# A vision block on one core: the opening's products, its copies, and the last choice of experts put in another order

## The chip, the cores and the metric

The program runs on one core of one Trainium2 chip. The metric is device time in microseconds (us) of one execution, lower being better. Times of single instructions come from one profiled execution.

## The reference

A tokeniser, one attention layer and one mixture-of-experts layer run over 32 images of 36 patches, so 1152 tokens of width 192.

```python
y = einsum('bchw,rc->bhwr', x, W_repr) + b_repr          # 3 channels to 5 representations
h = einsum('rbnp,rep->bne', patches(y), W_proj) + b_proj.sum(0)
h = h + attention(layernorm(h))                          # 12 heads of 64, 36 tokens an image, softmax(8 q.k)
xt = layernorm(h)
gates = softmax(xt @ gate_w + gate_b); expert = argmax(gates)      # 8 experts
out = h + (gelu(xt @ w1[e] + b1[e]) @ w2[e] + b2[e] of the chosen expert)
```

## The kernel before, in words

Each engine has its own instruction stream, written out by hand, and waits on semaphores; an engine works in order. A helper `own(ins)` makes DVE wait until its own instruction has written its result, and is used wherever the next one reads it. The tokens are nine tiles of 128, in three blocks of three tiles. Attention goes by units of two images (72 tokens), 16 in all.

- **Opening.** SP loads the projection weights, three tiles of x (`xb`), and the attention weights in pieces. DVE and ACT fold the 3-to-5 channel mix into one effective weight per channel: `weff[0]` by DVE alone, `weff[2]` and `weff[1]` from products that ACT scales. PE computes a bias row (`bias`), copied out by ACT. Then PE lays the bias into the accumulators of the three tiles (L667) and adds the channels 0, 2, 1 (L674). DVE takes the statistics of each tile (L1221 to L1223), POOL the reciprocal root (L1553), DVE normalises (L1125), PE turns the tile (L511, L512), ACT rounds it to fp32r (L939, L940) and copies its lower rows once more (L942), DVE takes the rest of the rounding (L1152, L1153). Then come the twelve query and key products of block 0 (L523). In between PE multiplies small columns for the gate (L681, L689), and transposes of the identity (`keep_clock`, L646), whose results nobody reads, fill its waits. ACT also rounds the weight pieces (`round_wqA`, L917, and `round_wqB`, L922), and DVE splits off the remainder (L1159, L1165).
- **Blocks.** The functions `middle_block` of PE, ACT and DVE interleave the units' attention of a block with the tokenising, turning and products of the next. PE may only turn the probabilities of a unit (`turn_probs`, L574) when ACT has copied those of the unit before (`take_probs`, L978).
- **Last block.** When a tile's attention is done, PE projects it (L603); DVE adds the residual into `rows` (L1279) and the gate logits into `raw` (L1280), takes statistics, and normalises it (`finish_row`, L1125). Rows go to a table in HBM by DMA; the last tile is normalised by ACT (L1066), which also issues two DMAs (L1069): three tiles, then one. DVE chooses the expert of four tiles at once (`gate_logits`, L1307 and L1317, and `choose_experts`, L1330 to L1336), PE ranks the tokens (L612 to L628), DVE turns ranks into slots (L1352 to L1370, L1440), PE makes the token lists (L636), DVE writes them as integers (`ids`, L1445).
- **Experts.** POOL waits for the rows in the table and for `ids`, then gathers tokens by list (L1565), 16 tiles of 128. PE turns a gathered tile (`turn_x`, L838 and L839), multiplies up (`up`, L849 first half, L856 second half) and down (L878); `more_lists` (L829) makes the lists of the tiles 8 to 15. ACT does the gelu, DVE the copies.

## Time and profile before

| | us |
|---|---|
| three executions | 240.25, 242.35, 243.03; median 242.35 |
| the profiled execution | 241.82 |
| its span in the trace | 240.1 |
| TensorE busy in it | 223.4 (93%) |

The span runs from the first to the last instruction in the trace; the 1.7 us that the profiled execution's time is longer lie around it. A row of a timeline or chain begins with the time from the start of the span and the duration.

### The profile page before, as it was taken

How to read it: one execution, taken by the hardware profiler on the slowest of the kernel's cores; microseconds unless marked ns; L12 is line 12 of the kernel's file. 1: busy time of each engine (PE TensorE's matmuls, PEld its weight loads, DVE VectorE, ACT ScalarE, POOL GpSimd, SP SyncE). 2: the span in 40 equal slices, each digit the busy share in tenths (PEclk: the TensorE clock that was granted, in tenths of full speed). 3: DMA queues.
4: the chain of work that ended last, by engine and by line, in shares of the span. 5: the costliest groups of instructions: out<-in, count | busy, mean ns of one | idle time of the engine just before them, and what ended most of it. 6: DMA issues, size and time to landing. Idle time of an engine off the chain costs nothing.

```text
span 240.1 us, 7756 instructions
## 1 busy us (share of the span) xinstructions
PE 223.4 (93%) x3238; PEld 206.1 (86%) x3238; DVE 121.5 (51%) x390; ACT 116.1 (48%) x309; POOL 53.4 (22%) x84
## 2 busy tenths in 40 slices
PE   6999999998999999899998899789999999999990
PEld 5898998887999888799977789679999999999980
DVE  1878236993431798447289737872324324324310
ACT  2765555547265637544556650305235546646220
POOL 8201000021110012023000021170354354353131
PEclk9999799999999999999999999999999999999998
DMA  5999962325054240500813533331112212311000
GB/s 183 332 238 360 413 256 62 105 67 175 3 194 169 68 127 9 203 1 30 284 52 88 139 132 101 132 107 59 48 49 64 85 49 53 79 47 48 3 0 0
DMA packets 10055, 27.70 MB, mean 115 GB/s; under 512 B 2333, under 2 KB 4921, under 8 KB 9380
## 3 DMA queue, kind: packets, MB, share of 16 engines
q1 hardware_dynamic: 7636, 22.28, 28.9%
q0 software_dynamic: 1840, 4.13, 6.2%
q10 hardware_dynamic: 544, 0.79, 0.9%
q8 instruction: 26, 0.43, 0.7%
q14 instruction: 9, 0.07, 0.1%
HBM read 21.00 MB, written 3.34 MB: 101 GB/s over the span
## 4 chain that ended last, share of the span: by engine, by line
PE 74%; DVE 11%; DMA 4%; ACT 3%; issue 3%; POOL 1%; SPq 1%; DVEq 0%; POOLq 0%
PE psum L523 19%; PE psum L878 13%; PE psum L849 9%; PE psum L603 8%; PE psum L856 6%; PE psum L587 4%; PE psum L556 3%; PE psum L574 3%; DMA w1s<-xT 3%; PE psum L504 3%; PE psum L674 2%; DVE kT L1177 2%; DVE top L1176 2%; PE psum L838 2%; ACT w2s L978 1%
## 5 line engine op out<-in xcount | busy, mean ns | idle before, releaser
L878 PE MATMUL psum<-w2s,kT 128*128 128x192 f32 (+1 forms) x192 | 33.8, 327 | 0.0
L523 PE MATMUL psum<-xn_hi,wq_parts 128*128 128x384 f32 x108 | 32.2, 353 | 0.3 <-DVE w_r L1153 0.3
L878 PEld LDWEIGHTS psum<-w2s,kT 128*128 128x128 f32 x192 | 30.8, 190 | 0.1
L1552 POOL TENSOR_SCALAR veps<-mv 128x1 f32<-128x1 f32 x15 | 3.3, 221 | 116.9 <-DVE mv L1122 116.9
L1097 ACT ACTIVATE kT<-psum,w1s 128x128 f32<-128x128 f32 x48 | 13.2, 375 | 26.1 <-PE psum L856 26.1
L1576 POOL DMA_INDIRECT out<-oT,ids x16 | 16.2, 1010 | 42.9 <-DVE oT L1499 42.9
L523 PE MATMUL psum<-w_r,wq_parts 128*128 128x384 f32 x72 | 25.2, 350 | 0.0
L1481 DVE COPY qT<-psum 128x128 f32<-128x128 f32 x16 | 4.7, 291 | 33.3 <-PE psum L839 33.3
L1097 ACT ACTIVATE kT<-psum,late 128x128 f32<-128x128 f32 x48 | 13.2, 375 | 16.7 <-PE psum L856 16.7
L523 PEld LDWEIGHTS psum<-xn_hi,wq_parts 128*128 128x128 f32 x108 | 20.9, 197 | 0.4 <-ACT xn_hi L942 0.4
L603 PE MATMUL psum<-wo,oT 128*128 128x200 f32 x108 | 20.4, 339 | 0.5 <-issue 0.5
L603 PEld LDWEIGHTS psum<-wo,oT 128*128 128x128 f32 x108 | 18.0, 190 | 1.1 <-issue 0.6
L1176 DVE TENSOR_REDUCE top<-psum 100x12 f32<-100x432 f32 x16 | 9.6, 602 | 17.8 <-PE psum L556 17.5
L1565 POOL DMA_INDIRECT wq_in<-token_table,ids x16 | 15.7, 981 | 10.2 <-DVE ids L1445 5.5
L523 PE MATMUL psum<-wq_parts,xn_hi 128*128 128x384 f32 (+1 forms) x54 | 17.0, 369 | 0.6 <-issue 0.6
L646 PE MATMUL psum<-ident 128*128 128x128 f32 x102 | 14.1, 295 | 2.2 <-POOL ident L1526 1.8
L955 ACT ACTIVATE kT<-kT 100x432 f32<-100x432 f32 x16 | 9.0, 563 | 12.4 <-DVE kT L1177 11.7
L949 ACT COPY qT<-psum 128x384 f32<-128x384 f32 (+4 forms) x30 | 9.4, 354 | 11.6 <-PE psum L523 11.6
L646 PEld LDWEIGHTS psum<-ident 128*128 128x128 f32 x102 | 12.5, 152 | 2.5 <-POOL ident L1526 1.8
L523 PEld LDWEIGHTS psum<-w_r,wq_parts 128*128 128x128 f32 x72 | 14.1, 196 | 0.0
L949 ACT COPY kT<-psum 128x384 f32<-128x384 f32 (+4 forms) x30 | 9.4, 354 | 9.3 <-PE psum L523 9.3
L1499 DVE TENSOR_TENSOR oT<-psum,oT 128x192 f32<-128x192 f32 x16 | 5.7, 358 | 15.8 <-PE psum L878 15.8
(176 smaller groups left out, 447.3 us busy)
## 6 DMA issues: line engine op xcount, KB each, us to landing
w1s<-w_b SPq DMA_DIRECT2D x1, 3474.0 KB, 13.6
w1s<-xT SPq DMA_DIRECT2D x9, 384.0 KB, 4.5
late<-wq_in SPq DMA_DIRECT2D x24, 108.0 KB
w2s<-w SPq DMA_DIRECT2D x2, 1152.0 KB, 7.1
w2s<-w SPq DMA_DIRECT2D x1, 1728.0 KB, 7.0
w1s<-w_b SPq DMA_DIRECT2D x1, 1158.0 KB, 5.2
late<-w_proj SPq DMA_DIRECT2D x2, 480.0 KB, 4.0
b2s<-b SPq DMA_DIRECT2D x1, 768.0 KB, 15.0
```

Of the source, the lines that this page charges most:

```text
L523: mm = pe.matmul(dst, lhsT, rhs, start=(i == 0), stop=(i == len(parts) - 1))
L587: mm = pe.matmul(dst[DH * k:DH * (k + 1), c * GT:(c + 1) * GT], v[0:SPAN, u % V_SLOTS, j * DH:(j + 1) * DH], probsT[u % 2][:, j * GT:(j + ...
L603: mm = pe.matmul(dst[0:TT, 0:D + EXPERTS], oT[:, c, at:at + TT], wo[:, c, :], start=(c == 0), stop=(c == PAIRS - 1))
L646: pe.transpose(psum[:, bank, 0:P], ident[:, :], ident[:, :])
L849: pe.matmul(psum[:, 2 * p2 + c % 2, at:at + SLOT], w[:, c * P:(c + 1) * P], fxA[p2], start=(c < 2), stop=False)
L856: mm = pe.matmul(psum[:, 2 * p2 + c % 2, at:at + SLOT], w[half, FF + at:FF + at + P], fxB[p2][half, :], start=False, stop=(c >= FCH - 2))
L878: mm = pe.matmul(psum[:, Y_BANKS[j % 2], 0:D], hidT[j % 2][:, c * P:(c + 1) * P], w[:, :, c, :], start=(c == 0), stop=(c == FCH - 1))
L949: cp = act.copy((qT if w == "q" else kT)[:, c, to], acc(slot[0])[:, tokens])
L1097: ge = act.activation(hidT[p2][:, c * P:(c + 1) * P], psum[:, 2 * p2 + c % 2, c // 2 * P:(c // 2 + 1) * P], ACT.Gelu, bias=w1_of(j)[:, UP ...
L1176: own(dve.tensor_reduce(most, sc, AX.X, ALU.max))
L1565: pool.indirect_dma_start(out=xg[j % 4], out_offset=None, in_=table, in_offset=bass.IndirectOffsetOnAxis(ap=ids[:, j:j + 1], axis=0)).then ...
L1576: pool.indirect_dma_start(out=out, out_offset=bass.IndirectOffsetOnAxis(ap=ids[:, j:j + 1], axis=0), in_=yo[j % 4], in_offset=None, bounds ...
```

## The change

It reorders work in three places.

1. **Opening.** A tile of x has a semaphore of its own (`x_first[t]`), and channel 0 of a tile waits for that tile only. Four of the filling transposes go. The first matmul into an accumulator is now channel 0's; the bias is laid in between channel 2 and channel 1. The gate columns are spread between the turns of the three tiles (2, 2, 2 instead of 0, 2, 4). On ACT, rounding the lower rows of weight piece 1 (`round_wqB(1)`) moves from before the tokens to behind the copies of the turned tiles, and the doubled lower rows (`double_xnB`, the old L942) come one step later, behind the next tile's two copies.
2. **Middle blocks.** The same doubling comes behind the next `take_probs`. In every `take_o` DVE takes the statistics before the gate logits instead of behind them.
3. **The last block.** The choice of experts is made in three parts: tiles 0 and 1 together, before the third projection is ready, then tile 2, then tile 3. ACT normalises tile 2 as well as tile 3, so `shift` has two columns. The ranking of the block before (`place_tokens`) is taken apart and laid into waits. `ids` is written before the three small instructions that make slots (`slots_in_tiles`). In the experts' start, the second tile is turned inside the first `up`, between its halves, instead of before it.

The core of the diff:

```diff
             for t in range(NT):
-                sp.dma_start(xb[:, t, :, :], xT[t]).then_inc(x_here, 16)
+                sp.dma_start(xb[:, t, :, :], xT[t]).then_inc(x_first[t], 16)
...
-            pe.wait_ge(x_here, 16 * NT)
-            pe.wait_ge(sc_free, 1)
-            keep_clock(4, TR_BANK)
-            taken(pe, product("bias"))
-            for t in range(NT):
-                pe.matmul(into(product("tok", t))[0:TT, 0:D], ident[0:TT, 0:TT], bias[:, :],
-                          start=True, stop=False)
-            for c in (0, 2, 1):
+            def channel(c):
                 pe.wait_ge(weff_ready[c], 1)
                 for t in range(NT):
                     slot = product("tok", t)
+                    if c == 0:
+                        into(slot)
+                        pe.wait_ge(x_first[t], 16)
                     for i in range(2):
                         mm = pe.matmul(acc(slot[0])[0:TT, 0:D], xb[:, t, 2 * c + i, :],
-                                       weff[:, c, i, :], start=False, stop=(c == 1 and i == 1))
+                                       weff[:, c, i, :], start=(c == 0 and i == 0), stop=(c == 1 and i == 1))
...
+            channel(0)
+            channel(2)
+            taken(pe, product("bias"))
+            for t in range(NT):
+                pe.matmul(acc(product("tok", t)[0])[0:TT, 0:D], ident[0:TT, 0:TT], bias[:, :], start=False, stop=False)
+            channel(1)
...
             keep_clock(10, TR_BANK)
             turn_tokens(0)
-            turn_tokens(1)
             pe.wait_ge(gw_here, 48)
             pe.wait_ge(woT_here, 48)
             gate_columns(0, 2)
+            turn_tokens(1)
+            gate_columns(2, 4)
             turn_tokens(2)
-            gate_columns(2, PAIRS)
+            gate_columns(4, PAIRS)
...
+            def second_turn_and_lists():
+                turn_x(1)
+                more_lists()
             turn_x(0)
             keep_clock(6, TR_BANK)
-            turn_x(1)
-            up(0, more_lists)
+            up(0, second_turn_and_lists)
...
-            for i in range(2):
-                round_wqA(i)
-                round_wqB(i)
+            round_wqA(0)
+            round_wqB(0)
+            round_wqA(1)
...
+            def double_xnB(t):
+                toks = slice(t % NT * TT, (t % NT + 1) * TT)
                 act.wait_ge(xn_hi_ready, t + 1)
                 act.copy(xnB[DB:2 * DB, toks], xnB[0:DB, toks]).then_inc(xnB_ready, 1)
...
-            for t in range(NT):
-                take_xn_hi(t)
+            take_xn_hi(0)
+            take_xn_hi(1)
+            double_xnB(0)
+            take_xn_hi(2)
+            double_xnB(1)
+            double_xnB(2)
+            round_wqB(1)
...
-                for i0, i1 in ((0, NG - 1), (NG - 1, NG)):
-                    if i1 == NG:
-                        act.wait_ge(shift_ready, 1)
-                        act.activation(rows[:, i0, D:2 * D], rows[:, i0, 0:D], ACT.Identity, bias=shift[:, :],
-                                       scale=rstd[:, 1, i0:i0 + 1]).then_inc(rows_ready, 1)
+                for k, (i0, i1) in enumerate(((0, NG - 1), (NG - 1, NG))):
+                    act.wait_ge(shift_ready, k + 1)
+                    act.activation(rows[:, i1 - 1, D:2 * D], rows[:, i1 - 1, 0:D], ACT.Identity,
+                                   bias=shift[:, k:k + 1], scale=rstd[:, 1, i1 - 1:i1]).then_inc(rows_ready, 1)
...
                 take_o(r)
+                tiles_of_tokens(b - 1)
                 finish_row(r)
                 take_o(r + 1)
+                own(slots_of_tokens(b - 1))
+                centre_logits(b, 0, 2)
+                dve.sem_inc(small_free, 1)
                 finish_row(r + 1)
-                place_tokens(b - 1)
+                own(scale_logits(b, 0, 2))
+                choose_experts(b, 0, 2)
                 take_o(r + 2)
                 take_o(r + 3)
-                finish_row(r + 2)
-                gate_logits(b)
-                choose_experts(b)
+                normed(1, r + 2)
+                shift_of(n - 2)
+                centre_logits(b, 2, 4)
+                own(scale_logits(b, 2, 3))
+                choose_experts(b, 2, 3)
+                ins = scale_logits(b, 3, 4)
+                own(ins)
+                shift_of(n - 1)
+                choose_experts(b, 3, 4)
+                dve.sem_inc(onehot_ready, 1)
...
-                tiles_of_tokens(b)
+                count_tiles(b)
                 dve.wait_ge(ids_full, 1)
                 dve.tensor_scalar(ids[:, 0:EXPERTS], psum[:, IDS_BANK, 0:EXPERTS], -1.0, float(TOKENS), ALU.mult,
                                   ALU.add).then_inc(ids_ready, 1)
+                slots_in_tiles(b)
```

`rank_tokens(b - 1)` now stands before the last `soften`. `centre_logits` is the first loop of the old `gate_logits` for some of the tiles (L1307), `scale_logits` the second (L1317), and `shift_of` the old `shift` instruction (L1313) for one tile. `count_tiles` is L1365 and L1367; `slots_in_tiles` is L1368 to L1370. In `take_o` the addition into `rows` is now waited for, the statistics follow, and the logits' addition, which frees the accumulator, is last.

## Rows read from the trace of the kernel before

**Rows 1.** The page, the chain that ended last: shares by engine

```profile
PE 74%; DVE 11%; DMA 4%; ACT 3%; issue 3%; POOL 1%; SPq 1%; DVEq 0%; POOLq 0%
```

**Rows 2.** The chain in order of time (start, us, what): opening, and block 1's products

```profile
11.85 4.56 PE psum L674 x28
...
22.16 12.32 PE psum L523 x60
...
65.08 11.43 PE psum L523 x65
```

**Rows 3.** Timeline of DVE, opening: start, us, operation, then idle and its releaser

```profile
7.09 2.58 DVE L1203 SCALAR_TENSOR_TENSOR w2s<-late,wr_br,w2s 128x384 f32<-128x384 f32 x4
...
11.16 0.56 DVE L1215 TENSOR_TENSOR w2s<-w2s 128x384 f32<-128x384 f32 x1
...
13.82 0.56 DVE L1215 TENSOR_TENSOR w2s<-w2s 128x384 f32<-128x384 f32 x1
...
15.01 0.69 DVE L1165 TENSOR_TENSOR wq_parts<-wq_in,wq_parts 64x512 fp32r<-64x512 f32 x1
...
19.41 0.38 DVE L1125 TENSOR_SCALAR rows<-h,mv,rstd 128x192 f32<-128x192 f32 x1 [0.22 <-POOL rstd L1553]
...
21.64 0.27 DVE L1153 TENSOR_TENSOR w_r<-psum,xn_hi 64x128 fp32r<-64x128 f32 x1
```

**Rows 4.** Timeline of ACT, opening

```profile
15.96 1.04 ACT L922 CAST wq_parts<-wq_in 64x1024 fp32r<-64x1024 f32 x1
...
21.43 0.30 ACT L942 CAST xn_hi<-xn_hi 64x128 fp32r<-64x128 f32 x1
```

**Rows 5.** Timeline of PE, opening

```profile
10.21 0.66 PE L646 MATMUL psum<-ident 128*128 128x128 f32 x4 [0.39 <-DMA w1s<-xT]
...
18.96 0.33 PE L511 MATMUL psum<-ident,rows 128*128 128x128 f32 x1 [0.17 <-DVE rows L1125]
...
20.14 0.96 PE L681 MATMUL psum<-gwA,w2s 128*128 128x8 f32 x8
```

**Rows 6.** DMA issues around 9.8 us: size, us from issue to landing

```profile
w2s<-w_outT SPq DMA_DIRECT2D x2, 96.0 KB, 7.5
```

**Rows 7.** Busy times of a stretch; behind POOL's the granted clock

```profile
23.00:27.00 4.00, 4.00 (x16) 4.00 (x15) 1.26 (x2) 1.44 (x3) 0.00 (x0) 0.57 1.11 450
```

**Rows 8.** Timeline of all engines, second middle block

```profile
95.78 0.65 PE L574 MATMUL psum<-ident,kT 36*36 36x36 f32 x48
...
96.75 1.04 ACT L978 COPY late<-psum 36x432 f32<-36x432 f32 x2
...
97.93 0.64 PE L574 MATMUL psum<-ident,kT 36*36 36x36 f32 x48 [0.61 <-ACT late L978]
```

**Rows 9.** The chain in order of time, first middle block and the last block's end

```profile
55.76 0.49 issue
...
148.53 0.36 DVE rows L1279
...
152.69 0.20 DVE onehots L1336
...
154.94 0.17 DVE none L1368
...
155.38 0.09 DVE ids L1445
...
155.53 0.74 issue
```

**Rows 10.** Timeline of ACT, last block's end

```profile
151.60 0.34 ACTq L1069 DMA_DIRECT2D token_table<-rows  x1
```

**Rows 11.** DMA issues from 148 to 166 us: size, us from issue to landing

```profile
token_table<-rows ACTq DMA_DIRECT2D x1, 192.0 KB, 2.8
```

**Rows 12.** Timeline of PE, the experts' start

```profile
159.92 0.82 PE L646 MATMUL psum<-ident 128*128 128x128 f32 x6
160.80 0.33 PE L838 MATMUL psum<-ident,wq_in 128*128 128x128 f32 x1
```

94 lines of the change are left out of this document (54 added, 40 removed).

## The prediction

> **What bounds the kernel now.** I read the page's chain first: TensorE carries 74% of it [rows 1]. So an edit pays only where PE waits or does work that goes away. I then followed the chain in order of time and marked where it leaves PE. In the opening it goes over PE's products (to 16.41), then statistics, turning and rounding, until the twelve query and key products begin at 22.16 [rows 2]. In the middle blocks it crosses ACT's copies of the probabilities [rows 8]. In the last block, from 148.53, it runs over DVE, POOL and a DMA until the first gather starts at 155.53 + 0.74 = 156.27 [rows 9]. From 161 us on PE does the experts without a gap, so whatever the experts start earlier is kept to the end. The three edits touch these three places.
>
> **The opening.** What is removed: four filling transposes, and PE's wait for all of x (0.39 us idle to 10.21, so PE was free at 9.82) [rows 5]. Channel 0 needs `weff[0]`, ready at 7.09 + 2.58 = 9.67 [rows 3], and one tile of x at a time, the last at 10.21. Its first product starts at about 9.8. A product of 192 columns is two instructions of 4.56 / 28 = 0.163 us [rows 2]. Channel 0 takes 12 of them, to 11.76, just behind `weff[2]` at 11.72; channel 2 goes to 13.72; the bias (6 instructions) to 14.70, past `weff[1]` at 13.82 + 0.56 = 14.38 [rows 3]. Moving the bias between the channels so covers that wait; without it PE would stand 0.66 us. Four instructions of channel 1 finish tile 0 at 14.70 + 0.65 and a tail of about 0.16, 15.5; before it was 16.41 [rows 2]. The products are 0.9 us earlier, but now DVE is late: it splits a weight piece until 15.70 [rows 3] and can begin the statistics there, 0.03 later than its work allows at most. Statistics began at about 16.44, so the gain is 0.74 to 0.76; tiles 1 and 2 are ready 0.65 us apart and DVE takes 0.68 for each, so it stays so. ACT would have been the next thing late: it rounds `round_wqB(1)` until 17.00 [rows 4], and must copy tile 0 at about 16.5. That is what moving this rounding is for; it is worth 0.5 us of the 0.76.
>
> The third normalising ran from 19.41 [rows 3]; it moves to 18.65, and the first turn from 18.96 [rows 5] to 18.2. Then the new order on PE: two turns' instructions (0.29), two pairs of gate columns of four instructions each at 0.96 / 8, about 0.11 net [rows 5], 0.44 each, between the turns. So tile 1 is turned by 19.36, later in its own chain than before, and tile 2 by 20.09. On ACT the copies of tile 2 end at 20.53, doubling 1 and 2 at 0.30 each [rows 4] at 20.73 and 21.02. The doubling no longer stands behind a wait for the copy just made, but PE hands over the turned tiles more slowly; the two nearly cancel. DVE's last remainder, 21.91 before [rows 3], ends at 21.04. PE started 0.25 behind it, so the products begin at 21.29 instead of 22.16: **0.87 us**. The new wait in it is that for the gate weights, reached at 18.5 and now ahead of the turn of tile 1, with everything behind it on PE. The last of these transfers was issued at about 9.8 and took 7.5 [rows 6], 17.3: 1.2 us of cover. Of `round_wqB(1)`: done by 22.05, its split (1.2 us more on DVE) by 23.5, wanted by the fifth product, at 0.88 us a product [rows 2] not before 24.8; 1.3 us of cover. SP's loads for block 1 wait on the normalised tiles and go 0.8 us earlier; nobody waits for them before 44 us. Ends for this term: 0.4, if DVE and ACT give back half; 1.0, if the whole lead of the products came through.
>
> **The middle blocks.** In the second block ACT starts the copy of unit 3's probabilities at 96.75 though PE had them at 95.78 + 0.65 = 96.43, and PE waits until 97.93 [rows 8]. With the doubling behind this copy, ACT is free at about 96.46: **0.29 us**. The doubling then falls into ACT's idle time while PE projects. For the third tile it stands behind one more copy and ends some 1.0 us before PE asks. In the first block a stall of 0.49 us in PE's own stream [rows 9], which no engine explains, let PE's result come as late as ACT was free; I count nothing there. Ends: 0 and 0.6. The statistics ahead of the logits' addition save 0.1 us of a path that PE covers here, and hold the accumulator 0.7 us longer, which its next user, at least one projection of 2.2 us away, doesn't notice.
>
> **The last choice.** The statistics of the last tile are not sped up much: the waited addition saves the 0.08 us of the logits' addition. What changes is behind the reciprocal root, ready at about 150.7. Before, DVE scaled four tiles (0.63), took the maximum (0.22), four levels (0.68), the choice (0.22) and the one-hots, until 152.69 + 0.20 = 152.89 [rows 9]. Now tiles 0 and 1 were chosen before, during the projection, and tile 2 while POOL works: shift at 149.6, centring two tiles to 150.03, scaling 0.18, and four steps of 0.2 end at 150.99. That is 0.3 later than the root, so DVE is the bound and not POOL. Tile 3 alone is scale, shift, maximum, level, choice, one-hot, six small steps: 152.05. So the ranking starts **0.84 us** earlier. Rank, list and counting follow as before; PE's filling ends at 151.9, just in time. `ids` then leaves out three instructions, from 154.94 to 155.29 [rows 9], **0.35 us**. Together ids would be ready at 155.47 - 1.19 = 154.28. The parts of `place_tokens` fall in DVE's idle times of 1.0, 1.5 and 1.1 us, and cost nothing; if that cover were gone they would cost their 2.4 us on DVE, but PE's projections end after it.
>
> **The new late thing** is the table. POOL waits for both row DMAs. The second was issued at 151.60 [rows 10] and landed 2.8 us later [rows 11], at 154.40, a full us before ids. Now tile 3's shift comes behind tile 2's choice, 151.35 instead of 150.99, so this DMA is issued at 151.96 and lands at 154.76. That is after the 154.28 of ids. With the same 0.81 us from the last wait to the gather (155.47 to 156.27), the gather starts at 155.60: **0.67 us**, not 1.19. Ends: 0.4 (the landing slower by 0.3), 1.19 (the landing doesn't bind). The Trainium skill (DMA: Bandwidth & Descriptors, Anatomy of one DMA) gives a fixed 2.0 us and the bytes at 436 GB/s; by it, an estimate of 2.45 us for 192 KB, the landing would be at 154.4 and the gain 1.0. The row has the measured 2.8, so it decides.
>
> **The experts' start.** PE filled until 160.74 and turned the second tile at 160.80 [rows 12]; now `up` begins at once when the filling is issued, at 160.67 in the old times, and the second turn is covered. **0.13 us**, ends 0 and 0.4 (when the second gather lands late).
>
> Sum: 0.87 + 0.29 + 0.67 + 0.13 = 1.96 us. Against the profiled execution, 241.82, that is 239.9. The median shown is 0.5 us above it; from 242.35 the same sum gives 240.4, which I take.
>
> **Rivals.**
>
> *The rows' DMA doesn't bind.* If it lands a little sooner, or POOL's 0.81 us overlaps with the wait, the gain is 1.19 there: 239.9. For it speaks that the 0.81 is nothing any row explains; against it the 1 us by which the two edges now pass each other. 0.13.
>
> *The clock in the opening's wake.* In 23 to 27 us TensorE was granted a mean of 0.57 of its 2.4 GHz, that is mostly 1.2 GHz [rows 7]. Twelve products took 12.32 us [rows 2]; at the 5 x 11.43 / 65 = 0.88 us that each takes in block 1, 10.55. So 1.76 us hang on it. It fell after four and a half us of turns and 8-column products; that stretch stays as long and as thin. If the change let the fall miss the products, 238.6: chance 0.10. If a second fall came, for instance in the waits before the gather, 242.2: 0.08. The Trainium skill (TensorE: Matmul & The Clock Gate, What's actually happening) says that the gate's timing isn't tied to the kernel's start, so the same code meets it differently. One trace can't show that; the 2.8 us between the three executions leave room for it, and I widen the range for it.
>
> *The opening gives its gain back.* If the turns spread by the gate columns, or the lists on ACT, cost what the products gained, 0.2 remains of the 0.87: 241.1. It would show as PE idle between the turns. 0.15.
>
> *Slower: the table's wait takes over.* The gather now hangs on a DMA issued later. If the write meets other transfers and takes the 7.5 us of the opening's crowded queue [rows 6], it lands at 159.46, the gather starts at 160.3, 4.0 us later than before, and the sum is -2.7: 245.1. It decides from a landing of 4.8 us on, where the sum is nothing. Against it: 2.8 measured on a queue of its own [rows 11]. 0.04.
>
> *It doesn't do what it says:* DVE's order leaves the choice no earlier, since the small steps cost the same for one tile as for four (0.2 each). Then 0.84 goes, and with it only the 0.67: 241.0. 0.03.
>
> **How the numbers follow.** The forecast has 0.47. Its own ends, 0.4 + 0 + 0.4 + 0 and 1.0 + 0.6 + 1.19 + 0.4, give 239.2 to 241.6. The range takes in the clock's two cases: 238.6 to 242.3. One per cent, 2.4 us, is about what a measurement of this kernel can tell from no change, and the forecast is below it. Faster by over 1% are the clock's miss, half of the first rival and the upper end of the forecast: 0.27. Slower by over 1% is the table's wait: 0.04. The rest, 0.69.
>
> **What would show it.** In the profile after: tile 0's statistics at 15.7; the first query product at 21.3; no wait of PE for the gate weights; ACT's copy at the second block right at PE's end; the one-hots 3.5 us after the last row's addition instead of 4.4; the last `ids` before the second row DMA lands; the gather 0.8 us after that landing; `up` before the second turn. I am wrong if a granted clock below 1 stands anywhere but once after the opening, if DVE is not free at 150.7, or if the first gather follows ids and not the rows.

## The result, and the profile after

| | before | changed |
|---|---|---|
| median | 240.82 us (20 executions) | 240.03 us (20 executions) |
| lowest, highest | 238.82, 243.77 | 237.34, 245.41 |
| ratio | | 0.993, 95% interval 0.9901 to 0.9959 |
| profiled execution, its span | 241.82, 240.1 | 239.32, 237.5 |

Each ratio in this document compares the executions within 1.5% of their kernel's fastest, here 18 of the 20 before and 12 of the 20 changed. By it the changed kernel is 0.7% faster, 1.7 us of 240.8, with an interval that excludes no change, and 0.3 us under the forecast gain of 1.96 us. Over all twenty executions the gain is smaller and doesn't stand clear of the noise: the medians are 0.8 us apart, the means 0.7, and the changed kernel spreads more (standard deviation 2.2 us against 1.2). A second measurement of it, changed_again below, has 2.3 us between the medians of all executions. The sum came out near; of its terms only some did, so each is read by itself.

The chain's shares in the changed kernel's page, beside those of [rows 1]:

```profile
PE 79%; DVE 8%; ACT 4%; issue 3%; DMA 3%; POOL 0%; SPq 0%; DVEq 0%; POOLq 0%
```

Its chain in order of time (start, duration, what), the pieces that answer to [rows 2] and [rows 9]:

```profile
15.99 0.38 DVE stats L1246
...
21.55 10.79 PE psum L523 x60
...
144.31 0.37 DVE rows L1304
...
...
150.44 0.75 issue
151.19 2.80 DMA wq_in<-token_table,ids
153.99 1.83 issue
155.82 0.33 PE psum L845
```

The statistics start at 15.99 (forecast 15.70), the query products at 21.55 (21.29), and the gather 151.19 - 144.31 = 6.88 us behind the last row's addition (before 7.74). Then comes a piece that nobody forecast: the gather's packets are there at 153.99, but PE turns the tile only 1.83 us later, and no engine explains it.

PE's timeline of the changed kernel, from the opening to the first turn of the experts (start, duration, engine, line, tiles, count, and in brackets the idle time ahead and what ended it); it answers to [rows 5] and [rows 8]:

```profile
5.48 4.08 PE L657 MATMUL psum<-late,wr_br 128*128 128x192 f32 x20 [0.44 <-DMA late<-w_proj]
10.01 4.17 PE L671 MATMUL psum<-w2s,w1s 128*128 128x192 f32 x24
14.02 1.14 PE L680 MATMUL psum<-bias,ident 128*128 128x192 f32 x6
...
18.51 0.33 PE L511 MATMUL psum<-ident,rows 128*128 128x128 f32 x1 [0.32 <-DVE rows L1150]
...
92.87 0.65 PE L574 MATMUL psum<-ident,kT 36*36 36x36 f32 x48
...
94.75 0.64 PE L574 MATMUL psum<-ident,kT 36*36 36x36 f32 x48 [0.33 <-ACT late L993]
...
127.08 0.65 PE L574 MATMUL psum<-ident,kT 36*36 36x36 f32 x48 [0.15 <-issue]
...
149.95 3.91 PE L646 MATMUL psum<-ident 128*128 128x128 f32 x34
...
155.82 0.33 PE L845 MATMUL psum<-ident,wq_in 128*128 128x128 f32 x1 [1.96 <-issue]
```

The new order of the opening is plain: channels 0 and 2 in one run of 24 instructions, the bias, channel 1; no wait of PE for x and none for the gate weights. In the block ACT starts its copy at 93.56, when PE has the probabilities (92.87 + 0.65 = 93.52); before it was 0.3 late. The last three rows are used further below.

Windows of the changed kernel (length; busy time of PE, its weight load, DVE, ACT and POOL, with counts; granted clock, 1.00 being 2.4 GHz; share of the DMA engines; GB/s), beside the clock of [rows 7]:

```profile
21.00:26.00 5.00, 4.75 (x31) 4.68 (x30) 2.65 (x4) 3.46 (x8) 0.00 (x0) 1.00 1.09 429
...
157.00:158.00 1.00, 1.00 (x6) 1.00 (x6) 0.50 (x2) 0.00 (x0) 0.20 (x1) 0.50 0.40 146
```

In this execution the clock did not fall after the opening, but did at 156 to 161, at the start of the experts. The first of the clock's rivals came true in this profile, a fall came later as the second had it, and they cancel: the twelve products took 10.63 us instead of 12.16 (1.5 won), and from the turn to the first gelu went 5.40 us instead of 4.11.

**One table for all kernels.** Times in us from each profile. "Statistics": from the first bias product (L657) to the first statistics. "Heads": from there to the first query product. "Block": from block 1's first query product to its first projection. "Last": from there to the last row's addition. "Gather": from that addition to the first gather. "Turn": from the gather to the turn of its tile. "Gelu": from there to the first gelu. From there to the end of the span all take 76.1 to 76.5. One stretch has no column, from the first query product to block 1's first: 40.2 to 41.0, and 41.8 to 42.6 in the three profiles whose clock fell after the opening (before, gates_back, both_mends).

| kernel | L657 | statistics | heads | block | last | gather | turn | gelu |
|---|---|---|---|---|---|---|---|---|
| before | 3.85 | 10.99 | 5.72 | 33.73 | 50.03 | 7.74 | 3.38 | 4.11 |
| changed | 4.08 | 10.51 | 5.56 | 33.42 | 49.00 | 6.88 | 4.63 | 5.40 |
| changed_again | 3.49 | 10.23 | 5.57 | 33.45 | 49.32 | 6.87 | 4.57 | 3.89 |
| opening_only | 4.46 | 10.89 | 5.56 | 33.70 | 48.99 | 7.75 | 3.26 | 4.28 |
| choice_only | 4.19 | 10.95 | 5.73 | 33.72 | 50.04 | 6.88 | 3.26 | 4.33 |
| old_second_turn | 3.5 | 10.29 | 5.55 | 33.41 | 53.43 | 6.88 | 3.19 | 4.43 |
| before_less_four | 4.5 | 11.42 | 5.73 | 33.71 | 49.48 | 7.81 | 3.32 | 4.15 |
| bias_copy_last | 3.49 | 10.20 | 5.56 | 33.44 | 49.00 | 6.88 | 4.47 | 3.91 |
| late_second_rows | 3.80 | 10.33 | 5.56 | 33.44 | 49.39 | 7.28 | 3.51 | 3.90 |
| fewer_fillers_tail | 4.02 | 10.81 | 5.57 | 33.47 | 49.00 | 6.90 | 3.35 | 4.21 |
| both_mends | 3.5 | 10.37 | 5.56 | 33.43 | 48.97 | 6.88 | 3.25 | 4.30 |
| rounding_back | 4.0 | 10.42 | 5.56 | 33.43 | 50.52 | 6.88 | 4.30 | 3.90 |
| gates_back | 3.49 | 10.20 | 5.36 | 33.42 | 49.27 | 6.88 | 4.52 | 3.90 |
| bias_first | 3.98 | 10.73 | 5.56 | 33.42 | 54.47 | 6.88 | 4.16 | 3.90 |

Two profiles of one kernel (changed and changed_again) agree within 0.1 us in most columns; "statistics" moves by 0.28 with the start, "last" by 0.3 with a stall of PE, and "gelu" by 1.5 when a clock fall lies in it.

### The profile page after: what moved, and what is told of

Same layout as the page of the kernel before. It is cut to its first block, busy times and chain, and to the rows that moved or that the text cites. A ratio compares the mean times of both kernels' runs of the same rounds, so it can differ in the third digit from the quotient of the medians.

```text
span 237.5 us, 7769 instructions
## 1 busy us (share of the span) xinstructions
PE 222.6 (94%) x3234; PEld 205.8 (87%) x3234; DVE 122.6 (52%) x396; ACT 116.5 (49%) x310; POOL 53.4 (22%) x84
## 4 chain that ended last, share of the span: by engine, by line
PE 79%; DVE 8%; ACT 4%; issue 3%; DMA 3%; POOL 0%; SPq 0%; DVEq 0%; POOLq 0%
PE psum L523 19%; PE psum L885 13%; PE psum L856 10%; PE psum L603 8%; PE psum L863 6%; PE psum L504 5%; PE psum L587 4%; PE psum L574 4%; PE psum L556 4%; PE psum L845 2%; PE psum L657 2%; DMA late<-w_proj 2%; DVE top L1201 1%; ACT w2s L993 1%; DVE kT L1202 1%
## 5 line engine op out<-in xcount | busy, mean ns | idle before, releaser
L523 PE MATMUL psum<-xn_hi,wq_parts 128*128 128x384 f32 x108 | 31.1, 342 | 0.3 <-ACT xn_hi L957 0.3
L523 PE MATMUL psum<-w_r,wq_parts 128*128 128x384 f32 x72 | 24.4, 339 | 0.0
L603 PE MATMUL psum<-wo,oT 128*128 128x200 f32 x108 | 20.4, 340 | 0.0
L523 PEld LDWEIGHTS psum<-xn_hi,wq_parts 128*128 128x128 f32 x108 | 20.0, 188 | 0.3 <-ACT xn_hi L957 0.3
L603 PEld LDWEIGHTS psum<-wo,oT 128*128 128x128 f32 x108 | 18.0, 190 | 0.7 <-issue 0.2
L523 PE MATMUL psum<-wq_parts,xn_hi 128*128 128x384 f32 (+1 forms) x54 | 16.9, 367 | 0.0
L646 PE MATMUL psum<-ident 128*128 128x128 f32 x98 | 13.5, 295 | 1.8 <-POOL ident L1577 1.8
L523 PEld LDWEIGHTS psum<-w_r,wq_parts 128*128 128x128 f32 x72 | 13.5, 188 | 0.0
```

Of the source, the lines that this page charges most:

```text
L523: mm = pe.matmul(dst, lhsT, rhs, start=(i == 0), stop=(i == len(parts) - 1))
L603: mm = pe.matmul(dst[0:TT, 0:D + EXPERTS], oT[:, c, at:at + TT], wo[:, c, :], start=(c == 0), stop=(c == PAIRS - 1))
L646: pe.transpose(psum[:, bank, 0:P], ident[:, :], ident[:, :])
```

## The experiments

**The parts by themselves.** The theory was the forecast's sum; the rival, that a whole part is worth nothing or costs time. Four kernels ran on one chip: the changed kernel once more; the kernel before with the opening's edits alone; the kernel before with the edits of the choice alone, on all engines, and the statistics ahead of the logits (without the doubling's move and the experts' start); and the changed kernel with the old order of the second turn.

changed_again has no edit. opening_only is the changed kernel with its last block and experts' start as before, and in the blocks the doubling in its old place:

```diff
                     if i < 2:
                         take_xn_hi(n + i)
+                        double_xnB(n + i)
...
                 take_xn_hi(n + 2)
+                double_xnB(n + 2)
                 take_attended(u + 4)
```

choice_only is the complement: opening, doubling and experts' start as before, the choice in three parts. old_second_turn, against the changed kernel:

```diff
-            up(0, second_turn_and_lists)
+            turn_x(1)
+            up(0, more_lists)
```

> The changed kernel once more, for what its executions share. If the stall of 1.96 us ahead of the first turn and the clock's fall at 157 us belong to the change, the profile shows both again. If they are chance (my theory), the first up is done 7.3 us behind the first gather's start, as before, and not 9.9. Ratio 0.993 again.

> Only the opening of the change (x by tile, bias between the channels, gate columns spread, ACT's order there); middle blocks, choice and experts' start as before. My theory, that the parts add up: 0.9 us less than before (ratio 0.996), and in the trace the first query product 0.9 us earlier measured from the first of PE's bias products (before: 22.16 - 5.45 = 16.71; changed kernel: 21.55 - 5.48 = 16.07 with 0.26 of late bias products in it). Rival, the clock: the opening's new order changes how often the clock falls in the query products; then the ratio is 0.99 or less, and the twelve products take 10.8 us and not 12.3.

> Only the choice of experts in three parts, with ids ahead of the slots and statistics ahead of the gate logits; opening, middle blocks' copies and experts' start as before. My theory: from the last row's addition to the first gather 6.9 us as in the changed kernel (before 7.74), 0.8 us less time, ratio 0.9965. Rival, the table's wait: the gather starts 0.8 us behind the landing of the second row DMA and not behind ids; it shows as a gather later than 7.0 us from the addition.

> The changed kernel with the second gathered tile turned before the first up, as before. My theory: the order is worth 0.1 to 0.4 us; the 1.96 us stall of PE at the first gathered tile and the fall of the clock behind it, seen in the changed kernel's profile, are chance and have nothing to do with this edit. Rival: putting the turn inside up brings them; then this kernel is 1 us or more faster than the changed one and its profile has neither.

Measured: changed_again 238.53 us against 240.80, ratio 0.9927 (0.9895 to 0.9959); opening_only 239.70, 0.9940 (0.9910 to 0.9969); choice_only 239.12, 0.9951 (0.9923 to 0.9979); old_second_turn 239.12, 0.9908 (0.9876 to 0.9940). changed_again has the late turn again (4.57) and no fall of the clock there, so the delay wasn't chance, as both forecasts held; the fall may be.

*The choice* gives 0.86 us in its trace (7.74 to 6.88), and by the ratio 1.2 us (0.5 to 1.9). Of the changed kernel, DVE's timeline between the addition and the last three small instructions:

```profile
145.36 0.15 DVE L1348 SCALAR_TENSOR_TENSOR shift<-mv,rstd 128x1 f32<-128x1 f32 x1
...
146.27 0.23 DVE L1362 SCALAR_TENSOR_TENSOR level<-lg,lgmax,order 128x8 f32<-128x8 f32 x1
...
146.93 0.23 DVE L1341 SCALAR_TENSOR_TENSOR lg<-lg,rstd,gate_bias 128x8 f32<-128x8 f32 x1
147.19 0.16 DVE L1348 SCALAR_TENSOR_TENSOR shift<-mv,rstd 128x1 f32<-128x1 f32 x1
...
147.92 0.17 DVE L1366 TENSOR_TENSOR onehots<-level,chosen 128x8 f16<-128x8 f32 x1
...
150.20 0.17 DVE L1495 TENSOR_SCALAR ids<-psum 128x8 uint32<-128x8 f32 x1
150.28 0.16 DVE L1401 TENSOR_SCALAR none<-nth 128x4 f32<-128x4 f32 x1
```

The one-hots end at 148.09, 3.78 behind the addition (before 4.35): 0.57, not 0.84. The first steps are as forecast (shift 1.05 behind the addition, 1.07 forecast). The forecast was too low for the four instructions of 8 columns that multiply and add (L1341, L1362), which stand alone and take 0.23 each; in the group of four tiles before they came at 0.65 / 4 = 0.16. `ids` stands in front of `none`, and gives 6.92 - 0.57 - 6.06 = 0.29.

ACT's timeline of the changed kernel (its copy in the second block, and the issues of the two writes of rows), and its DMA view (the queue of PE's instructions: packets, MB, share; the writes: KB, us from issue to landing):

```profile
93.56 1.04 ACT L993 COPY late<-psum 36x432 f32<-36x432 f32 x2
...
146.12 0.41 ACTq L1094 DMA_DIRECT2D token_table<-rows  x1
...
147.97 0.34 ACTq L1094 DMA_DIRECT2D token_table<-rows  x1
```

```profile
q8 instruction: 26, 0.43, 0.8%
...
token_table<-rows ACTq DMA_DIRECT2D x1, 576.0 KB, 3.0
...
token_table<-rows ACTq DMA_DIRECT2D x1, 192.0 KB, 1.9
```

The second write lands at 147.97 + 1.9 = 149.87, 0.5 us before ids (150.37). So the table does not bind, and the gather keeps all that ids gave. In the three kernels with the old last block the landing is 2.8 [rows 11], in the eleven profiles with the new one 1.9. Waiting behind the first write can hardly be the reason: the two are issued 1.62 to 1.67 us apart in the three and 1.84 or 1.85 here, and in late_second_rows, 2.82 apart, it is 1.9 as well. Something else differs. In those three, and in none of the eleven, an 8 KB packet of a queue of instructions starts 1.2 us behind the issue of the second write, and the write's last packets end at 2.3 to 2.4 us instead of 1.5. The DMA view of the kernel before, 152.8 to 153.2:

```profile
q14 instruction: 1, 0.01, 4.8%
```

No run moved this packet by itself, so the cause of the 2.8 stays open. The Trainium skill (DMA: Bandwidth & Descriptors, Anatomy of one DMA) gives its 2.0 us and the bytes for a DMA issued by GpSimd; ACT issues this one, so the forecast's estimate of 2.45 us by it doesn't apply, and the trace has 1.9 and 2.8.

*The opening* gives 1.4 us by its ratio, but not all of it where it was forecast: its statistics are only 0.10 earlier than before, though behind bias products that took 0.6 longer, its heads 0.16 faster. What else? The column "last": 48.99 against 50.03, though nothing of the last block is changed in it. *The second turn* shows in two columns with opposite signs: against the old order, "gelu" is up to 0.5 shorter in the changed kernel, "turn" 1.2 to 1.4 longer.

**Where the microsecond of the last block comes from.** PE's timeline of the kernel before:

```profile
130.18 0.62 PE L523 MATMUL psum<-wq_parts,xn_hi 128*128 128x392 f32 x2 [0.60 <-issue]
...
134.25 1.68 PE L603 MATMUL psum<-wo,oT 128*128 128x200 f32 x9 [0.51 <-issue]
```

"Issue" says that PE waited for nothing that the profile shows. Both stalls are in choice_only too (0.60 and 0.49), and neither in opening_only. A theory: they are PE's own instructions arriving late, and where the stream is cut depends on how many lie ahead; the opening's edit takes four filling transposes out. The rival: they follow from the opening's timing, and taking out the four alone changes nothing.

```diff
             pe.wait_ge(sc_free, 1)
-            keep_clock(4, TR_BANK)
```

> The kernel before, only without the four filling transposes ahead of the bias product. Theory: the two stalls of PE of 0.6 and 0.5 us in the last block (130.2 and 134.3 us in the kernel before, at the same places in the choice-only kernel, in none with the changed opening) belong to where PE's instruction fetches fall in its stream, and eight instructions fewer move them; from the first projection of block 1 to the last row's addition 49.0 us and not 50.0, the opening 0 to 0.4 us shorter, ratio 0.995. Rival: they belong to the new order of the opening; then 50.0 us here and a ratio of 0.998 to 1.0.

Measured: 239.99 us, ratio 0.9980 (0.9943 to 1.0017), not to be told from the kernel before; "last" is 49.48, halfway between theory and rival. Its PE timeline has one stall left of the two:

```profile
132.65 1.01 PE L603 MATMUL psum<-wo,oT 128*128 128x200 f32 x5 [0.43 <-issue]
```

Before, this stall lay behind the third of a projection's twelve matmuls (nine follow it); now it lies behind the seventh (five follow): four later, as many as were taken out. The other, between the second and third matmul of an L523, would by that stand ahead of the next L574; there PE doesn't wait in this profile. So the place goes with the stream, not with the opening's timing. The DMA view above fits: 26 packets of 0.43 / 26 MB, 16 KB each, for 3234 matmuls and as many weight loads, one for some 250. All kernels with the new opening have their stalls at the same three places, ahead of L574, behind the seventh matmul of an L603 (once the sixth), and at the head of a unit's L587, as bias_first's PE timeline shows:

```profile
10.35 1.24 PE L678 MATMUL psum<-bias,ident 128*128 128x192 f32 x6 [0.41 <-ACT bias L923]
...
127.47 0.64 PE L574 MATMUL psum<-ident,kT 36*36 36x36 f32 x48 [0.45 <-issue]
...
131.39 1.18 PE L603 MATMUL psum<-wo,oT 128*128 128x200 f32 x6 [0.59 <-issue]
...
136.66 1.71 PE L587 MATMUL psum<-w2s,late 100*64 100x72 f32 x24 [1.66 <-issue]
```

But their length isn't fixed: 0.15, 0 and 0 in changed, 0.28, 0.43 and 0.69 in rounding_back, 0.68, 0.16 and 1.79 in old_second_turn, none over 0.15 in opening_only, bias_copy_last, fewer_fillers_tail and both_mends. So "last" is 0.6 to 1.1 us shorter than before in eight of the eleven profiles with the new opening, and longer in three (rounding_back, old_second_turn, bias_first), where the stalls sum to 1.4, 2.6 and 2.7 us; the last two are profiles of long executions, 241.4 and 242.9 us.

The packets' times settle what PE waits for nearly as well as an experiment. The fourteen traces have 29 stalls with "issue" behind 20 us, besides one of 0.3 us at an L587 that all share. Each of the 29 ends 1.1 to 1.5 us behind the end of a 16 KB packet of that queue, wherever it lies and whether it lasts 0.15 or 1.96 us; the shared one, 1.6 to 5.8 us behind one, is something else. So PE goes on a fixed time after its instructions have come, and a late packet makes the stall. In bias_first the packet is there from 134.4 to 135.3, and PE, idle since 135.0, goes on at 136.66. In bias_first and old_second_turn, with the longest ones, this packet lies within the copy of the experts' weights. The DMA view of bias_first, 133 to 136 us:

```profile
q1 hardware_dynamic: 120, 1.01, 82.9%
q8 instruction: 1, 0.02, 2.0%
```

In the changed kernel the packets lie at 131.7 and 136.1, at both ends of that copy. That speaks for a fetch held up by other traffic, but it is two profiles; what makes a packet late was not settled.

**The opening's own term.** The theory after the first runs: the statistics hang on DVE's split, as forecast, but that on ACT's scalings of channel 1, these on the copy of the bias ahead of them, and that on PE's twenty bias products, whose duration changes from run to run. Then the copy behind the scalings of channel 1 instead of channel 2 should make the gain independent of it:

```diff
-                if c == 2:
+                if c == 1:
                     slot = product("bias")
```

> The changed kernel, but ACT copies the bias out behind channel 1's five scalings and not ahead of them. Theory: in the changed kernel DVE's statistics hang on ACT's channel-1 scalings, which stand behind the bias copy, which waits for PE's bias products; these take 3.5 to 4.5 us as PE's clock comes up sooner or later, so the gain of the opening varies from 0.1 to 0.9 us. Then here the statistics begin about 10.0 us behind PE's first bias product in any execution (15.5 in the span), also where the bias products take over 3.8 us, and the query products about 5.6 later; 0.4 us less than the changed kernel on average. Rival: the bias now comes later than PE wants it between channels 2 and 1 (13.7), and PE stands there; the statistics begin later than 15.5.

Measured: 240.12 against 241.56, ratio 0.9881 (0.9779 to 0.9984), from three executions and too wide to tell it from the changed kernel. Its profile happened on short bias products (3.49), where PE binds anyway, so the case it was made for was not seen. DVE's statistics in it, and the same instruction in changed_again:

```profile
15.91 0.37 DVE L1246 BATCH_NORM_STATS2 stats<-psum 128x6 f32<-128x192 f32 x1 [0.56 <-PE psum L671]
```

```profile
15.50 0.37 DVE L1246 BATCH_NORM_STATS2 stats<-psum 128x6 f32<-128x192 f32 x1 [0.34 <-PE psum L671]
```

DVE idles 0.56 where it idled 0.34, so the copy's move frees DVE by about 0.2, and the bound is then the products. In the table the dependence itself is plain: statistics minus L657 is 6.42 to 6.53 in the four profiles where DVE doesn't idle ahead of the statistics (changed, opening_only, rounding_back, late_second_rows), with L657 at 4.08, 4.46, 4.0 and 3.80. It isn't the only one: in fewer_fillers_tail L657 is 4.02, but PE waits 0.34 us for `weff[0]`, starts channel 0 at 10.18 (9.57 in changed_again), and the statistics follow 5.93 behind that start in both. Behind the range of L657 lies this, in opening_only's PE timeline:

```profile
1.80 3.25 PE L646 MATMUL psum<-ident 128*128 128x128 f32 x14 [1.80 <-POOL ident L1544]
5.46 4.46 PE L657 MATMUL psum<-late,wr_br 128*128 128x192 f32 x20 [0.42 <-DMA late<-w_proj]
```

Late in the changed kernel 34 of the same transposes take 3.91 us (its timeline above). The same transpose takes 3.25 / 14 = 0.23 us at the start and 3.91 / 34 = 0.115 later, twice as fast; yet the granted clock is given as 1.00 in both. Windows of the changed kernel (the last of the values in front of the DMA share is the clock):

```profile
3.00:4.00 1.00, 1.00 (x7) 1.00 (x6) 0.00 (x0) 0.00 (x0) 0.94 (x2) 1.00 0.64 196
151.00:152.00 1.00, 1.00 (x12) 1.00 (x11) 0.96 (x5) 0.00 (x0) 0.81 (x1) 1.00 0.00 0
```

Seven matmuls in the first of them and twelve in the second; at 157, where 0.50 is granted, it is six of the same size. So PE starts at the pace of the lower level, though the record says 1.00. And the windows of L657 alone in opening_only (length, busy time of PE and its weight load, clock) show where it speeds up:

```profile
5.50:7.30 1.80, 1.80 (x6) 1.80 (x7) 1.00 0.98 355
7.50:9.30 1.80, 1.80 (x13) 1.80 (x13) 1.00 0.98 377
```

The bias products start 0.32 us apart at first and 0.163 later. In opening_only the seventh is the first fast one, in changed the fifth, and in the profiles with 3.49 all are fast: that is the whole range of L657.

Three kernels then undid one edit each of the changed one. rounding_back, the rounding of weight piece 1:

```diff
             round_wqA(1)
+            round_wqB(1)
...
             double_xnB(2)
-            round_wqB(1)
```

gates_back, the gate columns:

```diff
             turn_tokens(0)
+            turn_tokens(1)
...
             gate_columns(0, 2)
-            turn_tokens(1)
-            gate_columns(2, 4)
             turn_tokens(2)
-            gate_columns(4, PAIRS)
+            gate_columns(2, PAIRS)
```

bias_first, the place of the bias (with `start` moved to it from channel 0, and `into` in place of `acc`):

```diff
+            taken(pe, product("bias"))
+            for t in range(NT):
+                pe.matmul(into(product("tok", t))[0:TT, 0:D], ident[0:TT, 0:TT], bias[:, :], start=True, stop=False)
             channel(0)
             channel(2)
-            taken(pe, product("bias"))
-            for t in range(NT):
-                pe.matmul(acc(product("tok", t)[0])[0:TT, 0:D], ident[0:TT, 0:TT], bias[:, :], start=False, stop=False)
             channel(1)
```

> The changed kernel with ACT's rounding of the lower rows of weight piece 1 back ahead of the tokens. My forecast put 0.5 us on moving it: ACT would be late for tile 0's copy, and the third normalising and the query products 0.5 us later behind the statistics (6.1 instead of 5.56). The theory after the traces: it ends when tile 0's copy is due and the copies of tiles 1 and 2 have 0.36 us of idle each, so the query products come 5.6 us behind the statistics all the same.

> The changed kernel with the gate columns as before: turns 0 and 1, two pairs, turn 2, four pairs. PE's sum of work between the last channel and the query products is the same, and PE is busy in it without a gap: theory, the query products 5.4 to 5.6 us behind the statistics, as with the spread columns. Rival: the spread columns delay ACT's copies of tile 1; then 5.2 us or less here.

> The changed kernel with the bias laid in first, ahead of channel 0, as before, x still by tile. Theory: PE waits for ACT's copy of the bias, 0.6 us behind the last bias product, and then does the same 34 instructions to tile 0; the statistics come 0.1 to 0.5 us later than in the changed kernel, 10.6 to 10.9 us behind the first bias product, and more where the bias products are long. Rival: only the wait for all of x mattered; then 10.2 us as in the changed kernel.

Measured, one execution each: 238.74, 239.53 and 242.88 us; the times tell little, the columns do. *rounding_back*: statistics 10.42 (DVE-bound), heads 5.56, as in the changed kernel. Moving the rounding is worth nothing. ACT's timeline there shows why:

```profile
16.23 1.04 ACT L933 CAST wq_parts<-wq_in 64x1024 fp32r<-64x1024 f32 x1
17.18 0.52 ACT L943 COPY h<-psum 128x192 f32<-128x192 f32 x2
18.05 0.32 ACT L943 COPY h<-psum 128x192 f32<-128x192 f32 x1 [0.35 <-DVE veps L1248]
```

ACT copies the first tile 0.5 us late, as forecast, but the second right behind it, and it waits for the third; DVE normalises only when it has the statistics of all three. *gates_back*: heads 5.36 against 5.56. Spreading the gate columns costs 0.2. *bias_first*: statistics 10.73. At the same L657 DVE alone would allow 10.42 (rounding_back), so the bias between the channels is worth 0.3, by one profile each. Its PE timeline, shown above, has the place: PE waits 0.41 us for the copied bias at 10.35. Its long time comes from elsewhere, the three stalls (2.7 us) and a granted clock of 0.50 from 136 to 143.

**The table's wait.** Does POOL ever hang on the second write of rows? If tile 3's shift comes behind its choice, the write goes later and the choice a little earlier:

```diff
                 ins = scale_logits(b, 3, 4)
                 own(ins)
-                shift_of(n - 1)
                 choose_experts(b, 3, 4)
                 dve.sem_inc(onehot_ready, 1)
+                shift_of(n - 1)
```

> The changed kernel with tile 3's shift behind the choice, so that ACT issues the second row DMA about 0.9 us later, 148.9 instead of 148.0. This is the wait that I had forecast to bind. In the changed kernel it landed 0.5 us ahead of ids. Theory: the landing, 1.9 us from its issue, comes 0.3 to 0.5 us behind ids now, and the gather starts 0.8 us behind the landing: 7.2 to 7.4 us from the last row's addition instead of 6.88. Rival: the gather's 0.8 us is POOL's own preparation and overlaps with the landing; then 6.9 us.

Measured: 238.50 us, ratio 0.9889 (0.9793 to 0.9985). ids is 5.99 us behind the addition (6.06 before), but the gather 7.28 instead of 6.88, and POOL's timeline names what it waited for:

```profile
152.02 1.10 POOL L1616 DMA_INDIRECT wq_in<-token_table,ids  x1 [5.07 <-DMA token_table<-rows]
```

and ACT's timeline of the same kernel says when that was issued:

```profile
149.37 0.34 ACTq L1094 DMA_DIRECT2D token_table<-rows  x1
```

149.37 + 1.9 is 151.27, and the gather starts 0.75 behind it. So the mechanism of the forecast is real; the change as it stands misses it by 0.5 us.

**The late turn.** In the changed kernel the gather's tile is turned 1.2 us later than before, behind a stall of 1.96 that nothing explains. Theory A: the order of the second turn itself delays it, through something that PE's stream waits for. Theory B: again PE's instructions, because another cut of the stream falls there. The DMA view of the changed kernel at 152.9 to 153.4:

```profile
q0 software_dynamic: 21, 0.10, 73.0%
q8 instruction: 1, 0.02, 17.4%
```

A packet of PE's instructions runs beside those of the gather; 17.4% of 16 engines over 0.5 us is one engine for 1.4 us. To tell the theories apart, the new order stays and fourteen filling transposes of the last block go. A second kernel has the bias copy moved as well.

```diff
-                keep_clock(14, TR_BANK)
+                keep_clock(9, TR_BANK)
                 taken(pe, product("o", r + 2))
                 first_lists(0, KNOWN)
-                keep_clock(14, TR_BANK)
+                keep_clock(9, TR_BANK)
...
-            keep_clock(34, TR_BANK)
+            keep_clock(30, TR_BANK)
```

> The changed kernel with 14 filling transposes fewer in the last block's end (14, 14 and 34 become 9, 9 and 30), that is 28 instructions of PE fewer ahead of the first gathered tile. Theory: the first gather lands 1.3 us late in the changed kernel (4.6 us from its start to the turn instead of 3.3) because a 16 KB fetch of PE's instructions runs on the same DMA engines at that moment; with the stream shorter the fetch falls behind the turn, and the turn comes 3.3 us behind the gather, ratio 0.988. Rival: the turn of the second tile inside up makes the first gather late by itself; then 4.6 us again. A risk of both: the clock falls while PE stands idle longer, which would show as a granted clock of 0.5 and a first up of over 6 us.

> The changed kernel with both mends: 14 filling transposes fewer in the last block's end, and ACT's bias copy behind channel 1's scalings. Theory: turn 3.3 us behind the first gather, statistics about 10.2 us behind PE's first bias product and not on DVE's splits, also where the bias products take over 3.8 us; ratio 0.985 to 0.987, 0.3 us under the kernel with fewer fillers. Rival: the bias copy moves nothing, since the clock's rise at the start also delays PE's own products; then statistics at 10.2 only where the bias products were short, and the ratio of the fewer fillers.

Measured: fewer_fillers_tail 237.99 against 241.56, ratio 0.9864 (0.9796 to 0.9931); both_mends, which moves the bias copy as well, 237.80 against 241.22, 0.9881 (0.9836 to 0.9927). "Turn" is 3.35 and 3.25, as with the old order. In fewer_fillers_tail the fetch has moved to 157.4, behind the turn:

```profile
q8 instruction: 1, 0.02, 16.4%
```

Theory A falls as it was put: the order is the same and the delay is gone. But the order has a part in it. With the old one none of five profiles has a packet between gather and turn, old_second_turn among them, whose stream ahead of the turn is that of the changed kernel; with the new one all seven with the full filling have it. Why, no run shows. Six profiles have the delay (changed, changed_again, bias_copy_last, rounding_back, gates_back, bias_first), and in each the packet comes about 1.75 us behind the gather and the turn another 2.4 to 2.9 behind the packet. From the packet's end to the turn it is 1.27 to 1.48 us in all six, and 1.46 in late_second_rows, where the gather starts 0.4 later and the packet does not (1.1 behind it); the packets themselves last 0.9 to 1.4. These are the 1.1 to 1.5 us of the other stalls. So the turn's own instructions, or some just ahead of it, come with this packet, and the turn waits for them; with 14 fewer instructions ahead they are in the one before. A slower gather beside the packet would not keep that distance, and is the weaker reading. Only that the queue is PE's is inferred, from the count of its packets.

both_mends had short bias products once more (3.49); its statistics, at 10.37, are not earlier than in changed_again, so the copy's move shows no gain in either kernel with it, and the case of long products stays unseen.

One more thing is in the table: without the delay "gelu" is 4.21 and 4.30, as with the old order. From the gather to the first gelu go 7.56 and 7.55 us; with the old order 7.47 to 7.62 in five kernels. The new order alone is worth nothing. With the delay the two columns make 8.06 to 8.46, a loss of 0.5 to 0.9.

The thinner filling has a price in the clock, in that kernel's windows:

```profile
149.00:153.00 4.00, 3.68 (x32) 3.35 (x30) 3.47 (x17) 1.37 (x2) 1.10 (x1) 0.59 0.19 68
```

The granted clock fell to 0.5 here, but in the transposes that nobody waits for, and was back before the turn. A fall in the changed kernel at 156 hit the first `up`. These two have the lowest medians of all; their intervals overlap the changed kernel's, so only against the kernel before is the gain settled.

## Why the prediction was right, and where it wasn't

The gain was forecast at 1.96 us and is 1.7; three terms were off and two were missing, and they nearly cancel. That the sums agree is luck in part. Changed_again against the profile of before, clock fall left out, has 0.76 + 0.15 + 0.28 + 0.71 + 0.87 - 0.97 = 1.80 us in the columns from "statistics" to "gelu". The 0.71 is PE's stalls, which no edit aimed at, and the -0.97 the late turn, which nobody forecast. By the signs that the prediction set for itself it was wrong twice: a granted clock below 1 stands at 156 and not after the opening, and the first gather follows ids and not the rows. In us, by the table, clock falls left out:

| step | forecast | measured |
|---|---|---|
| statistics of the opening | 0.74 to 0.76 | 0.4 to 0.5 at like L657; 0.48 and 0.76 in the two profiles of changed against before |
| behind the statistics | 0.11 | 0.16 |
| middle blocks | 0.29 | 0.3 |
| choice (one-hots) | 0.84 | 0.57 |
| `ids` ahead of three | 0.35 | 0.29 |
| the table's wait | -0.52 | 0 |
| experts' start | 0.13 | 0, and -0.5 to -0.9 by the late turn |
| PE's stalls in the last block | none | 1.0 in the changed profile, 0.7 in changed_again |

**The opening, 0.87.** "DVE is late: it splits a weight piece until 15.70": right, DVE bound the statistics in the changed profile. What failed is taking 15.70 as fixed. It hangs on the bias products through ACT, and these last 3.5 to 4.5 us. The old opening depends on them too, so like is to be set against like: choice_only and changed, with L657 at 4.19 and 4.08, have 10.95 and 10.51; before_less_four and opening_only, at 4.49 and 4.46, have 11.42 and 10.89. That is 0.4 and 0.5. The forecast 0.76 comes out only between before and changed_again (10.23), whose bias products were 0.36 shorter. Moving the rounding, "worth 0.5 us of the 0.76", was worth nothing: ACT is late for one tile only, and the normalising waits for the third. And the gate columns and the doubling "nearly cancel" was near: the columns cost 0.2, all the rest behind the statistics gained 0.36. With the 0.16 behind the statistics the opening gave 0.6 to 0.7 instead of 0.87.

**The middle, 0.29.** Right in place, mechanism and size: 33.73 to 33.42; opening_only and choice_only, which leave the blocks' doubling where it was, have 33.70 and 33.72.

**The choice, 0.67.** The steps were right, two terms mis-sized, one condition failed. One-hots gave 0.57 for 0.84, since such a lone instruction with 8 columns costs 0.23 and not 0.16 to 0.2. The table's landing was taken from one row, 2.8 us, which held 0.9 us of something that the change takes away; it is 1.9. (By its own numbers, 154.76 + 0.81, the forecast term was 0.70 and not 0.67.) This is the first rival, given 0.13, and with it the term is 0.86.

**The experts' start, 0.13.** Nothing of it is there. "The second turn is covered" is true, but the first gelu comes no sooner for it. And the turn now meets a fetch of PE's instructions, 0.5 to 0.9 us that no rival had; nor had one the stalls at 130 and 134, which stand as "issue" in the trace of before. The one such stall that the forecast named, 0.49 us in [rows 9], should have led to them.

**The clock.** Of the fourteen profiles seven have a granted clock of 0.5 for 3 to 7 us ahead of the end: before, gates_back and both_mends within 21 to 27, old_second_turn and bias_first within 136 to 143, fewer_fillers_tail at 149, changed at 156. The fall after the opening, [rows 7], comes with the old opening and with the new one, and is missing with either. So neither clock rival is shown to be an effect of the change; whether the change makes falls or long stalls more frequent, which its wider spread would allow, one profile of each kernel can't say.

**Slower by the table's wait** did not come: the landing would have had to be 0.5 us later to bind, and 1.9 is far from the 7.5 of [rows 6].

## What to carry to other kernels

A wait without a releaser in an engine that has thousands of instructions ("issue") can be a cost of where the stream is cut: an edit that adds or removes a few instructions moves it, here by 1 us either way, as much as the edits themselves were worth; so try a handful more or fewer fillers before judging an order. A landing time is to be read with what else ran on the DMA engines at the time, and a short instruction's cost from a row in which it stands alone. And a milestone early in a kernel is worth nothing until what fixes it, followed back to the first product, is known to be steady between executions.

## What the hardware showed that was not expected

- The same filling transpose takes 0.23 us in the first 5 us and 0.115 later, while the records give a granted clock of 1.00 for both; 0.50 granted at 157 goes with the pace of the start. In these fourteen profiles the record doesn't show the start's slower pace.
- PE's instructions come in packets of 16 KB, each for some 250 instructions, and one holds a DMA engine for 0.9 to 2.1 us. At the seams between them PE stood 0 to 2.0 us, in different executions of nearly the same stream, and each of 29 such stalls ended 1.1 to 1.5 us behind the end of a packet.
- In three profiles the granted clock fell within or up to 1.3 us behind a PE stall of 1.66 to 1.96 us; five idle times of 1.50 to 1.89 us ahead of the late turn have none behind them (bias_first, rounding_back, bias_copy_last, gates_back, changed_again). The Trainium skill (TensorE: Matmul & The Clock Gate, Part 4) says of TensorE's transpose mode that it doesn't count as work for the clock gate in the same way. In the changed kernel 34 transposes in a row, 0.115 us each, ran for 3.9 us at a granted clock of 1.00, which fell 3.0 us behind them, 1.1 behind the stall; with 14 fewer in the block it fell within them. No run here shows whether such transposes count less.
- A write of 192 KB to HBM landed 1.9 us after its issue in eleven profiles, 1.84 to 2.82 us behind the write ahead of it, and 2.8 in the three that had a packet of instructions beside it.
